# Products into an unread bank ahead of each expert phase, four result buffers, stores on ScalarE's DMA queue

## The reference, cut to what matters

```python
logits_fk = einsum('bsd,nd->bsn', x @ W_fk + b_fk, emb_fk_n)     # likewise logits_rk
w_fk, _ = topk_sparsify(softmax(logits_fk), 4)                   # w_rk the same
all_h   = einsum('bsd,ndr->bsnr', x, f_know)    # f_know: 128 matrices of 192 x 128
h       = einsum('bsnr,bsn->bsr', all_h, w_fk)
all_out = einsum('bsr,nrd->bsnd', h, r_know)    # r_know: 128 matrices of 128 x 192
out     = einsum('bsnd,bsn->bsd', all_out, w_rk)
```

## Time and profile before

| | us |
|---|---|
| median of 3 runs | 916.93 (914.58 to 917.58) |
| the profiled execution's own time | 910.85 |
| its span in the profile | 909.1 |
| TensorE busy in the span | 635.4 (70%) |
| ScalarE busy | 353.0 (39%) |
| matrix products of the expert phases (L1038), 1632 instructions | 257.4 |
| xsT copies on ScalarE (L1291), 136 | 63.3 |
| result copies of layer 0 (L1278), 68 | 40.2 |
| result copies of layer 1 (L1283), 136 | 58.4 |

### The profile page before, as it was taken

One profiled execution on the slowest core, in us unless ns is written; L12 is line 12 of the kernel. 1 busy time (PEld: TensorE's weight loads), 2 busy tenths in 40 slices (PEclk: granted clock), 3 DMA queues, 4 the chain that ended last, 5 costly groups with the idle time before them and its releaser, 6 DMA issues.

```text
span 909.1 us, 15402 instructions
## 1 busy us (share of the span) xinstructions
PE 635.4 (70%) x4404; PEld 509.7 (56%) x4405; DVE 378.0 (42%) x1332; ACT 353.0 (39%) x760; POOL 403.6 (44%) x397
## 2 busy tenths in 40 slices
PE   6698789898889817267999699995008886788100
PEld 6487677776767616135788588884005553455100
DVE  2844586877877998669300011100111101220132
ACT  4237365484745533251444223442004452445100
POOL 2335052350502157235730477731677724720475
PEclk9689999999986978576999658998559997999755
DMA  4261727547230718495764446764996865776432
GB/s 109 68 214 61 275 67 294 206 161 278 106 140 20 139 46 208 112 245 140 202 164 118 109 131 162 186 157 116 332 324 178 212 165 132 206 187 152 118 98 71
DMA packets 138029, 145.71 MB, mean 160 GB/s; under 512 B 11670, under 2 KB 121535, under 8 KB 137983
## 3 DMA queue, kind: packets, MB, share of 16 engines
q1 hardware_dynamic: 124606, 117.74, 46.6%
q0 software_dynamic: 13376, 27.41, 10.2%
HBM read 72.62 MB, written 72.50 MB: 160 GB/s over the span
## 4 chain that ended last, share of the span: by engine, by line
PE 43%; DVE 17%; DMA 13%; issue 10%; ACT 6%; SPq 5%; POOL 4%; ACTq 1%; POOLq 0%; DVEq 0%
PE bank L1038 21%; DMA wide_dram<-os 8%; PE bank L1027 5%; SPq L489 4%; POOL gat L629 3%; PE bank L814 3%; PE bank L769 3%; PE bank L799 2%; DVE pick L1707 2%; DMA xs<-mid_dram 2%; PE bank L754 2%; ACT os L1283 1%; PE bank L829 1%; DMA h_dram<-h 1%; PE bank L880 1%
## 5 line engine op out<-in xcount | busy, mean ns | idle before, releaser
L1038 PE MATMUL bank<-matrices,xsT 96*64 (+1 forms) x1632 | 257.4, 313 | 16.3 <-ACT xsT L1291 16.1
L1038 PEld LDWEIGHTS bank<-matrices,xsT 96*64 96x64 f32 (+1 forms) x1632 | 204.2, 147 | 53.9 <-issue 35.9
L629 POOL DMA_INDIRECT gat<-wide_dram,slots x152 | 146.0, 961 | 189.7 <-SPq L478 144.2
L1027 PE MATMUL bank<-ident,xs 128*96 128x128 f32 (+1 forms) x408 | 83.6, 319 | 91.3 <-DMA xs<-mid_dram 62.3
L1027 PEld LDWEIGHTS bank<-ident,xs 128*96 128x96 f32 (+1 forms) x408 | 49.1, 167 | 127.3 <-DMA xs<-mid_dram 61.2
L573 POOL TENSOR_TENSOR qk_sum<-qk_pad 64x888 f32<-64x888 f32 x16 | 27.6, 1726 | 202.0 <-ACT qk_pad L1115 182.4
L1753 DVE TENSOR_SCALAR acc<-gat,wts 128x128 f32<-128x128 f32 x19 | 5.8, 306 | 260.6 <-DMA gat<-wide_dram,slots 260.6
L616 POOL DMA_INDIRECT wide_dram<-x2b,slots x76 | 76.3, 1004 | 56.3 <-DVE slots L1714 35.0
L1291 ACT ACTIVATE xsT<-bank 96x512 f32<-96x512 f32 (+1 forms) x136 | 63.3, 482 | 84.3 <-PE bank L1027 83.9
L1283 ACT ACTIVATE os<-bank 64x384 f32<-64x384 f32 x136 | 58.4, 478 | 79.1 <-DMA wide_dram<-os 42.1
L1278 ACT ACTIVATE os<-bank 64x512 f32<-64x512 f32 x68 | 40.2, 590 | 120.9 <-PE bank L1038 120.9
(11 more groups left out here) (179 smaller groups left out, 861.5 us busy)
## 6 DMA issues: line engine op xcount, KB each, us to landing
wide_dram<-zeros SPq DMA_DIRECT2D x6, 3328.0 KB, 14.4
mid_dram<-zeros SPq DMA_DIRECT2D x8, 1664.0 KB, 18.6
xs<-wide_dram SPq DMA_DIRECT2D x68, 192.0 KB, 2.8
wide_dram<-os SPq DMA_DIRECT2D x68, 192.0 KB, 2.9
matrices<-in_L_ffn_f_know SPq DMA_DIRECT2D x8, 1536.0 KB, 17.6
matrices<-in_L_ffn_r_know SPq DMA_DIRECT2D x8, 1536.0 KB, 17.2
wide_dram<-os SPq DMA_DIRECT2D x68, 128.0 KB, 2.5
xs<-mid_dram SPq DMA_DIRECT2D x68, 128.0 KB, 2.9
```

The source lines that it names most:

```text
L629: pool.indirect_dma_start(gat[i][:, e, :], None, wide_dram[b], bass.IndirectOffsetOnAxis(ap=slots[:, t, k:k + 1], axis=0))\
L1027: last = pe.transpose(bank[r % 2][0:kp, c:c + ROWS], src, ident[:])
L1038: last = pe.matmul(out_bank[0:W, n * width:(n + 1) * width], xsT[r % 2][0:kp, c:c + W], matrices[0:kp, bass.ds(starts[(r * SB + k) * 2 + h ...
```

## The change: what it does

- **Products into an unread bank.** Ahead of the first `transposed` of each phase TensorE issues `WARM[ph]` = 12, 20, 12, 12 products of `ident` with `ones` (128x128 by 128x128, fp32) into bank 7, which nothing reads in these phases. Ahead of phase 2 there are 12 more, once the first six restore pieces have landed.
- **Four result buffers.** `os2` and `os3` are laid over the memory of `rank0`; the body r writes `os_[r]` and waits for the store of the same buffer one step earlier.
- **Stores by ScalarE.** `results` waits for its own copy and then issues the store itself. SyncE only loads.
- **Pieces in another order.** Feature piece 2 is issued in group 7 with three waits fewer, and piece 3 joins 4 to 7 at the end. The restore pieces keep their order; the first six count on a semaphore of their own.

```diff
+WARM = (12, 20, 12, 12)
...
-                    sp.wait_ge(cat_ready, 2 * GROUPS)
-                    sp.wait_ge(queries_filled, GROUPS)
-                    sp.wait_ge(v_filled, 4 * GROUPS)
-                    load_f(range(2, 4))
+                    load_f(range(2, 3))
...
             sp.wait_ge(res_used, GROUPS + 1)
             sp.wait_ge(stored, 32 * GROUPS + 1)
-            load_f(range(4, EXPERTS // CHUNK))
+            load_f(range(3, EXPERTS // CHUNK))
...
                 with sp.Fori(0, STEPS - 1) as s, sp.If(s + 1 < used):
                     for r in range(RING):
                         sp.wait_ge(t_filled[ph], s * RING + r + 1)
                         load(s + 1, r)
-                        store(s, r, s * RING + (RING + r + 1))
-                for r in range(RING):
-                    store(used - 1, r, used * RING + (r + 1))
                 for r in range(RING):
                     sp.wait_ge(y_stored[ph][r], used * 16 + 1)
...
-                sp.dma_start(dst, r_view[:, n:n + CHUNK, :]).then_inc(r_loaded, 16)
+                sp.dma_start(dst, r_view[:, n:n + CHUNK, :]).then_inc(r_first if n < 6 * CHUNK else r_loaded, 16)
...
+                for n in range(WARM[ph]):
+                    pe.matmul(bank[7][:, 0:ROWS], ident[:], ones[:], start=True, stop=True)
                 transposed(0, 0)
...
                 if ph == 2:
-                    pe.wait_ge(r_loaded, 16 * (EXPERTS // CHUNK))
+                    pe.wait_ge(r_first, 16 * 6)
+                    for n in range(WARM[0]):
+                        pe.matmul(bank[7][:, 0:ROWS], ident[:], ones[:], start=True, stop=True)
+                    pe.wait_ge(r_loaded, 16 * (EXPERTS // CHUNK - 6))
...
                 def results(s, r):
                     act.wait_ge(y_filled[ph], s * RING + r + 1)
-                    if r < 2:
-                        act.wait_ge(y_stored[ph][r + 2], 16 * s + 1)
-                    else:
-                        act.wait_ge(y_stored[ph][r - 2], 16 * s + 17)
+                    act.wait_ge(y_stored[ph][r], 16 * s + 1)
...
                     last.then_inc(y_copied[ph], 1)
+                    act.wait_ge(y_copied[ph], s * RING + (RING + r + 1))
+                    rows = wide_dram[b][bass.ds(s * (RING * SB * ROWS) + r * (SB * ROWS), SB * ROWS), 0:width]
+                    act.dma_start(rows.rearrange("(k p) d -> p k d", p=W), os_[r][:, :, 0:width])\
+                       .then_inc(y_stored[ph][r], 16)
```

More of the change, by code:

```diff
@@ L162, in tower @@
         x2b = sb("x2b", [ROWS, SPREAD, D])
-        rank = [sb("rank0", [ROWS, BATCHES[0][1], 2 * EXPERTS])]
+        rank = []
+        phase[0] = ExitStack()
+        rank.append(sb("rank0", [ROWS, BATCHES[0][1], 2 * EXPERTS]))
+        phase[0].close()
+        phase[0] = ExitStack()
+        os_late = [sb(f"os{i}", [W, SB * ROWS // W, D]) for i in (2, 3)]
+        phase[0].close()
+        phase[0] = ctx
+        rank0_room = sb("rank0_room", [ROWS, BATCHES[0][1], 2 * EXPERTS])
         phase[0] = ExitStack()
@@ L183, in tower @@
         xs = [sb(f"xs{r}", [ROWS, SB, D]) for r in range(RING)]
-        os_ = [sb(f"os{i}", [W, SB * ROWS // W, D]) for i in range(2)]
+        os_ = [sb(f"os{i}", [W, SB * ROWS // W, D]) for i in range(2)] + os_late
         xsT = [sb(f"xsT{i}", [128, SB * 256]) for i in range(2)]
@@ L326, in tower @@
         f_loaded = sem("f_loaded")
+        r_first = sem("r_first")
         r_loaded = sem("r_loaded")
@@ L452, in expert_rows @@
                 src, width = ((wide_dram[b], D), (mid_dram[b], RANK))[layer]
-                out_width = (RANK, D)[layer]
                 used = sp.value_load(steps_used[0:1, b, layer:layer + 1], min_val=1, max_val=STEPS)
@@ L462, in expert_rows @@
                     load(0, r)
[L463 to L467, removed]
                 with sp.Fori(0, STEPS - 1) as s, sp.If(s + 1 < used):
@@ L1272, in results @@
                     act.wait_ge(y_filled[ph], s * RING + r + 1)
-                    if r < 2:
-                        act.wait_ge(y_stored[ph][r + 2], 16 * s + 1)
-                    else:
-                        act.wait_ge(y_stored[ph][r - 2], 16 * s + 17)
+                    act.wait_ge(y_stored[ph][r], 16 * s + 1)
                     if layer == 0:
-                        last = act.activation(os_[r % 2][:, :, 0:width],
+                        last = act.activation(os_[r][:, :, 0:width],
                                               bank[2 + r][0:W, :].rearrange("p (n w) -> p n w", w=width), ACT.Copy)
@@ L1282, in results @@
                             src = bank[2 + 2 * (r % 2) + k][0:W, 0:2 * width].rearrange("p (n w) -> p n w", w=width)
-                            last = act.activation(os_[r % 2][:, 2 * k:2 * k + 2, :], src, ACT.Copy)
+                            last = act.activation(os_[r][:, 2 * k:2 * k + 2, :], src, ACT.Copy)
                     last.then_inc(y_copied[ph], 1)
+                    act.wait_ge(y_copied[ph], s * RING + (RING + r + 1))
+                    rows = wide_dram[b][bass.ds(s * (RING * SB * ROWS) + r * (SB * ROWS), SB * ROWS), 0:width]
+                    act.dma_start(rows.rearrange("(k p) d -> p k d", p=W), os_[r][:, :, 0:width])\
+                       .then_inc(y_stored[ph][r], 16)
                 with act.Fori(0, STEPS) as s, act.If(s < used):
```

## The result

| | before | after |
|---|---|---|
| median, us | 916.85 | 1031.2 (1026.4 to 1038.6, 4 runs) |
| ratio | | 1.1259 [1.1172, 1.1346] |
| the profiled execution's own time | 910.85 | 1038.55 |
| its span | 909.1 | 1036.5 |
| TensorE busy in the span | 635.4 | 736.0 |

Slower, as forecast, but by 114 us in place of 23: the median lies 91 us above the forecast and 71 above the upper end of its range.

What follows compares the result with a forecast made beforehand. TensorE bounds the four expert phases, waiting at step ends on ScalarE's copies and partly at the low clock. Terms 16.0 + 15.6 + 5.9 - 17.3 + 3.8 - 1.0 = +23.0 took the median to 940 us, range 919 to 960.

Steps and rivals of the forecast that it cites:

- (a): Layer 0 step ends, phases 0 and 1: ScalarE's store issue delays xsT by 1.07 us, 15 times: +16.0 us.
- (b): Layer 1 steps: ScalarE's stores with four buffers make a step 9.98 us against 8.94, 15 step ends: +15.6 us.
- (c): Phase 0's start: feature piece 3, now issued last, lands at 419.8; +5.9 us together with (d).
- (d): Unread products ahead of phase 0: 6.5 us on the path, but they raise the clock; +5.9 us together with (c).
- (e): Unread products ahead of phase 1: hidden in idle time, the clock holds high from its start, -17.3 us.
- were the clock even in trouble later, +10: Upper bound of (e), phase 1: the clock also in trouble later, +10 us instead of a gain.
- clock not held: Rival, chance 0.20: clock falls at phase 1's start, (e) gives nothing, 957 us; or at layer 1's step ends, +12.
- (f): Unread products ahead of phases 2 and 3: net +3.8 us for phase 2, 0 for phase 3.
- (g): Ends of phases 2 and 3: the last results wait for no store, -1.0 us together.

Runs made afterwards that it cites:

- e7: The kernel before with four result buffers and nothing else; 902.32 us, ratio 0.985.
- f4: The changed kernel with five more unread products at each layer 0 step end, between transposes and products; 951.2 us, ratio 1.0406.
- f1: The changed kernel with all result stores given back to SyncE; 893.58 us, ratio 0.977.
- e6: The kernel before with four result buffers and feature piece 3 issued behind the last hidden state; 903.82 us, ratio 0.993.
- g3: The changed kernel with stores on SyncE and ScalarE held at each layer 0 step end by four unused activations, each waiting for the previous; ratio 1.055.
- e1: The changed kernel with all result stores given back to SyncE, on a chip with slow first steps; ratio 1.0045.

## Why the prediction was wrong

The mechanism of the steps held. The step that failed is in (a): it priced a step end of layer 0 as 1.07 us of delay and put what the idleness does to the granted clock at nothing. That term was 93 us in the profiled executions and 80 in the medians.

**(a) Layer 0's step ends: right in kind, 5 us short.** The issue is 0.62 as taken. ScalarE's next xsT starts 1.90 us after results 3 (440.16 to 442.06), forecast 1.58: between the end of the issue and xsT lie 0.51, where 0.2 had been allowed. The step is 12.23 us against 11.88 forecast; 15 x 1.42 = 21.3 in place of 16.0.

**(b) Layer 1: right.** 10.16 us a step, forecast 9.98; 18.3 in place of 15.6. e7 adds what the sum had not separated: four buffers alone give 8.24, so the stores on ScalarE cost 1.92 a step and the buffers hide 0.70 of it.

The Trainium skill (Perfetto Trace Analysis, section DMA Optimizations) suggests one engine for loads and another for stores where there are loops, and gives no price. In this kernel the split does not pay: it costs 57.6 us with the clock held (f4 against f1). By the Trainium skill (Perfetto Trace Analysis, section DMA Instruction — HWDGE) the issuing engine is held until the descriptors are made. The trace agrees: ScalarE's issue takes 0.62 us.

**(c), (d) Phase 0's start: right.** The late piece costs 5.7 us alone (e6 against e7). With the products the third body stands 8.6 us later in the profiled execution, against 5.9 forecast; the pieces behind the last hidden state were issued 3.7 us later already (382.27 against 378.61), which is none of this step. Phase 0 does start at 1.96 us a group.

**(e) Phase 1: the start right by another way, the rest lost.** The unread products were to be hidden and to leave 1.2 us of idleness, which the clock would hold over. In fact 3.48 us of idleness stand ahead of them, they take about 6.1 us, the first transposes come 3.0 us later than before, and the granted clock is 0.74 over the products and 1.00 behind them: they brought it back, they did not hold it. Where the stores are SyncE's, the forecast stretch is there: in f1 the first transposes are at 524.61 and the third step's products at 547.68, 23.07 us where 23.3 was forecast, with 2.6 us more ahead of it. The 40.67 us that it was set against were those of one execution (23 and 8 us of low clock in e7 and e6, which have no unread products either). With ScalarE's stores, phase 1 loses its clock at the first step end. The bound "were the clock even in trouble later, +10" is the nearest that the sum came to that; phase 1 took 58.1 us more.

**The failed step, in (a).** Its step end was priced as 1.07 us of delay and nothing else. What was not asked is what TensorE's clock does under 2.07 us of idleness 15 times, though the rival "clock not held" did ask it for layer 1 ("the new step ends have 2.5", +12) and there was wrong: layer 1 ran at 0.98 and 0.97. In layer 0 that rival gave the clock only the -17.3 to lose and not the high clock that the kernel before had in all the rest of phases 0 and 1. The price of that is read between the changed kernel and f4: from the third body of phase 0 to its end 119.2 us against 89.1 (438.39 to 527.45), so 30; in phase 1 some 63 (172.4 from the first transposes, against 109.7); 93 in the profiled executions, 80 in the medians. With the clock held the sum would have been +33 (951.2 - 918.1), against +23.0.

The Trainium skill (TensorE: Matmul & The Clock Gate, section A second HAM failure mode: psum-queue depth-cycling) tells of a kernel whose short idle times between groups of products, because they came often, made the clock swing between its two levels. g3 agrees: at the high clock each idle time is at most 1.50 us, and the granted clock is 0.64 to 0.79 over the stretch, made of groups at 1.96 and at 3.67. So does phase 0 of the changed kernel, with idle times of up to 1.6 us and once 2.1, and 0.73. In phase 1 of the changed kernel it did not swing but stayed low. The rival with a chance of 0.20 had the right cause in the wrong places: its stakes were the start of phase 1 and the step ends of layer 1, and what was lost was the high clock of layer 0.

**(f), (g).** Phase 2: from the products behind the last piece to the second step 15.80 us (789.82 to 805.62), before 12.84; +3.0 against +3.8. (b) and (f) make 21.3 us, and all that follows phase 1 took 17.8 more, so 3.5 came back there; how much of it at the ends of phases 2 and 3 was not measured.

## What to carry to other kernels

An engine that copies for TensorE in a loop has no room for a transfer's issue where its next copy is what TensorE waits for; in this kernel one store in four, moved back, was worth 125 us. Price a new wait of TensorE twice, as its own length and as what the granted clock does to all products behind it, and take the stake from the rows at either level (1.96 against 3.67 us a group). Products that nobody reads, put into idle time that recurs, show whether a loss is the clock's (f4: 80 us of 138 came back); taking the idle time away was worth more (f1: all of it).

## What was not expected of the hardware

- In phase 1 of the changed kernel the clock, once low, stays low with TensorE busy for 141.5 of 154.5 us. The kernel before came back after 40 us, e7 after 23 and e6 after 8. In phase 0 of the changed kernel itself it came back five times (466.72, 483.66, 517.47, 541.75 and 548.09) and fell again at each step end that followed. What decides whether it comes back no run tells.
- Layer 1 kept 0.97 to 0.98 with 0.95 + 1.31 us of idleness at each step end, more than layer 0 lost its clock by. Its products use 128 rows where layer 0's use 96, and its steps are shorter; no run tells which of these matters, if either does.
- At a step end of layer 0 TensorE's own transposes start 0.3 to 0.7 us after the last products in the kernel before and in f1, and 0.5 to 0.95 in f4, all put down to "issue". Why they wait, and why longer there, stays open.
- On three of five chips the first pass through each phase's loop ran one product at a time, in e1 with 1.4 to 3.1 us between them and once 32.6 us of nothing, all put down to "issue", and every kernel that ran on both sorts of chip took over 200 us more. The steady steps were as elsewhere. Why stays open.
